# TensorE's order in a pipelined decoder layer: the gate projection split around a transpose, the query projection moved ahead of the gated scores

## The reference

```
x = x + gla(layernorm(x))             # gated linear attention, 16 heads
x = x + cross(layernorm(x), ctx)      # cross attention, 112 + 16 keys
x = x + moe(layernorm(x))             # 4 experts, top 2, capacity 512

gla:   q, k, v = x@Wq.T, x@Wk.T*s, x@Wv.T;  g = x@Wg.T + bg
       o = scan with decay over tokens (as blocked scores here), normed per head
       return silu(g) * o @ Wo.T
cross: q = ln_head(x@Wq + bq);  k, v from ctx, k normed per head
       return (softmax(q k) v, once for 112 keys, once for 16, added) @ Wo + bo
```

## Time and profile before

| | us |
|---|---|
| median of 3 runs | 1132.35 (1131.61 to 1132.56) |
| the profiled execution | 1131.85 |
| its span in the trace | 1130.1 |
| PE busy | 974.3 (86%) |
| DVE, ACT, POOL busy | 716.4, 470.1, 519.7 |
| mean granted clock of TensorE | 0.912 |

### The profile page before, as it was taken

How to read it: one execution, slowest core, us unless ns; L and a number is a source line. 1 busy time by engine, 2 the same in 40 slices (tenths; PEclk the granted TensorE clock), 3 DMA queues, 4 the chain that set the end, 5 groups by cost and what they waited for, 6 DMA issues and landing times.

```text
span 1130.1 us, 19117 instructions
## 1 busy us (share of the span) xinstructions
PE 974.3 (86%) x7225; PEld 570.4 (50%) x7225; DVE 716.4 (63%) x1397; ACT 470.1 (42%) x774; POOL 519.7 (46%) x610
## 2 busy tenths in 40 slices
PE   4699999999999999999999752107899999999994
PEld 2355666666666666666665432103344444444442
DVE  7677867877787778777876445622446446446572
ACT  4544564556555655555554324112233233233210
POOL 2446767666766676667666521277100000002642
PEclk9598999999999999999999875559899999999998
DMA  8340000000000000000000006155534334334583
GB/s 286 115 155 8 8 8 3 7 6 6 1 5 6 6 1 5 6 6 2 4 2 5 1 1 223 49 196 162 115 111 150 112 111 150 111 111 148 170 234 120
DMA packets 43644, 82.73 MB, mean 73 GB/s; under 512 B 12107, under 2 KB 12379, under 8 KB 43601
## 3 DMA queue, kind: packets, MB, share of 16 engines
q1 hardware_dynamic: 37328, 67.45, 18.7%
q0 software_dynamic: 6272, 14.71, 4.2%
HBM read 64.29 MB, written 22.04 MB: 76 GB/s over the span
## 4 chain that ended last, share of the span: by engine, by line
PE 57%; DVE 17%; issue 8%; POOL 7%; DMA 5%; ACT 3%; SPq 2%; POOLq 0%; DVEq 0%
PE ps L988 14%; PE ps L989 13%; PE ps L990 13%; PE ps L1080 5%; PE ps L994 4%; PE ps L1172 3%; POOL xg_scratch L691 3%; POOL xn_all L703 2%; DVE G L1431 2%; PE ps L1183 2%; DVE mx L1536 2%; PE ps L1203 2%; DVE sm L1549 1%; DVE big L1658 1%; DMA xn_all<-y_scratch,idx_get 1%
## 5 line engine op out<-in xcount | busy, mean ns | idle before, releaser
L703 POOL DMA_INDIRECT xn_all<-y_scratch,idx_get x32 | 37.3, 1165 | 257.2 <-DMA y_scratch<-big 241.7
L575 POOL TENSOR_TENSOR hrs<-hve,neg_half 128x16 f32<-128x16 f32 x48 | 139.9, 2914 | 3.8
L962 ACT ACTIVATE big<-ps 128x512 f32<-128x512 f32 x64 | 38.1, 597 | 223.4 <-PE ps L990 223.1
L988 PE MATMUL ps<-w2h,big 128*128 128x512 f16 x256 | 97.7, 381 | 11.0 <-DVE big L1328 11.0
L1723 DVE TENSOR_SCALAR big<-big 128x512 f16<-128x512 f32 x64 | 27.7, 432 | 119.8 <-ACT big L962 119.8
L988 PE MATMUL ps<-big,w1h 128*128 128x512 f16 x256 | 97.0, 379 | 1.5 <-DVE big L1328 1.5
L989 PE MATMUL ps<-w2l,big 128*128 128x512 f16 x256 | 97.5, 381 | 0.0
L990 PE MATMUL ps<-w2h,big 128*128 128x512 f16 x256 | 97.5, 381 | 0.0
L989 PE MATMUL ps<-big,w1h 128*128 128x512 f16 x256 | 97.0, 379 | 0.0
L990 PE MATMUL ps<-big,w1l 128*128 128x512 f16 x256 | 97.0, 379 | 0.0
L1080 PE MATMUL ps<-qeo,kt 32*128 32x64 f32 (+3 forms) x1024 | 72.0, 261 | 8.2 <-DVE scm L1478 8.2
(11 more groups left out here) (291 smaller groups left out, 2636.3 us busy)
## 6 DMA issues: line engine op xcount, KB each, us to landing
wst<-in_w SPq DMA_DIRECT2D x32, 1024.0 KB, 5.3
xg_scratch<-zero SPq DMA_DIRECT2D x16, 256.0 KB, 8.5
big<-xg_scratch SPq DMA_DIRECT2D x4, 1024.0 KB, 7.7
out<-x_all SPq DMA_DIRECT2D x4, 1024.0 KB, 8.7
pr<-in_w_attn SPq DMA_DIRECT2D x3, 1024.0 KB, 8.2
x_all<-in_w_attn SPq DMA_DIRECT2D x3, 1024.0 KB, 10.9
x_all<-in_x SPq DMA_DIRECT2D x1, 3072.0 KB, 11.4
y_scratch<-big SPq DMA_DIRECT2D x3, 1024.0 KB, 5.0
```

What stands on the lines that cost most here:

```text
L575: pool.tensor_tensor(hrs[n][:, :], hve[n][:, :], neg_half[:, :], ALU.pow).then_inc(hdev[n], 1)
L703: pool.indirect_dma_start(out=yg[b], out_offset=None, in_=y_dram, in_offset=bass.IndirectOffsetOnAxis(ap=idx_get[:, k, b:b + 1], axis=0), ...
L962: act.activation(hg[f % 2], psum[f % 2][:, 512:1024], ACT.Gelu, scale=UN).then_inc(hg_r, 1)
L988: nc.tensor.matmul(o, lh, rh, start=first, stop=False)
```

## The change

TensorE's body gets another order; no instruction is added or removed on any engine, and no other engine's order changes. `rows` takes the range of k slices, and gives its signal only with the last of them. `a1_g` is called twice, for k = 0, 1 and k = 2, 3, six matmuls each; `b1_x` comes between. `b1_q`, which was the second step of the next pass on `s[2]`, becomes the last step of the pass on `s[1]` (the same sequence), after `b2_logits` and ahead of the next pass's S0.

```diff
-            def rows(ps, xh, xl, col, done):
+            def rows(ps, xh, xl, col, done, ks=range(KC)):
 
-                for k in range(KC):
+                for k in ks:
                     last = mm3(ps, xh[:, k, :], xl[:, k, :], wh[:, k, col:col + D], wl[:, k, col:col + D], k == 0, k == KC - 1)
-                last.then_inc(done, 1)
+                if k == KC - 1:
+                    last.then_inc(done, 1)
...
-            def a1_g(s):
+            def a1_g(s, ks):
                 b, par, half = s
                 weights(b, 2)
                 after(pe, v_r, b)
-                rows(a1, xth, xtl, C_G, g_ps)
+                rows(a1, xth, xtl, C_G, g_ps, ks)
...
             def body(s):
                 on(s[1], a2_scores, 0)
-                on(s[2], b1_q)
                 on(s[3], b2_turn, 0)
                 on(s[1], a2_scores, 1)
...
                 on(s[3], b2_x3)
-                on(s[0], a1_g)
+                on(s[0], a1_g, range(KC // 2))
                 on(s[1], b1_x)
+                on(s[0], a1_g, range(KC // 2, KC))
                 on(s[3], b2_logits)
+                on(s[1], b1_q)
```

## The result

The changed kernel takes 1180.77 us (median of 4 runs, 1177.96 to 1185.87), the one before 1131.98 (median of 4). The ratio is 1.0441, interval 1.040 to 1.048: slower by 4.4%. The profiled execution took 1177.96 us, its span is 1176.1, against 1131.85 and 1130.1.

The account below looks back on a forecast made before the run. PE was taken as the bound, at half clock for a stretch in most passes. From 1131.85 us: plus 34 for the longer path, minus 21 for old falls, plus 35 for new ones, 1180 us; range 1148 to 1191.

Parts of the forecast that it names:

- b1_x waits: At b1_x, now six matmuls earlier in PE's list: PE idles 1.1 to 1.3 us for xn2, which comes unchanged.
- S1 waits for the mask: At a2_scores 1, covered only by transposes: about 1.1 us idle, 3.70 us from a2_scores 0 to it.
- The path at full clock: PE from b1_x to a2_scores 1: 9.10 us against 6.83, 2.27 us a pass longer, 34 us over 15 paths.
- The old falls go: Half-clock stretches of about 3.4 us, in b1_q: at best all 14 go away, 21 us back.
- New falls, over S1: Clock falls over a2_scores 1 and steps behind: 15 passes, two in three long (2.75 us), others 1.5: 35 us.
- What makes a fall long: A fall just before a2_scores 1 lasts 6.8 us, since that step leaves the clock down; full matmuls of b1_q raised it.
- short falls only: Rival: the clock falls in each pass but is back after 3.4 us: 1167 us, chance 0.30.
- no falls: Rival: dense b1_q next to the thin steps keeps the clock up: 1145 us, chance 0.14.
- the faster one: Rival: the clock stays up and xn2 is there when PE gets to b1_x: 1126 us, chance 0.03.

Follow-up runs that it names:

- e1: The changed kernel with b1_q put back to its old place, so that only the gate projection is split: 1138.64 us, ratio 1.0036 to the kernel before.
- e3: The changed kernel with four more full matmuls of 512 columns in PE's idle time between b2_turn 0 and a2_scores 1: 1141.14 us.
- e6: The changed kernel with eight more thin float32 matmuls (32 rows, 64 columns) between b2_turn 0 and a2_scores 1: 1194.98 us.
- e2: The kernel before with only b1_q moved to after b2_logits, the gate projection left whole: 1176.88 us, ratio 1.0387.
- e4: The kernel before with four more full matmuls of 512 columns ahead of a2_scores 0, where PE is never idle: 1134.72 us, ratio 1.0009.

## Why the prediction held, point by point

Forecast 1180, measured 1180.77, in the range. The direction rested on two waits that the rows of before already priced, and on where the clock would fall.

- *b1_x waits.* Forecast 1.1 to 1.3 us idle, measured 0.98. The reason held: six matmuls earlier in the list, `xn2` comes when it came, 2.82 us after the start of `b2_x3` (316.78 - 313.96), before 2.83 (334.01 - 331.18). e1 shows the price of the split on the pass, 0.86 us at full clock.
- *S1 waits for the mask.* Forecast S0 to S1 3.70 us with 1.1 idle, measured 3.65 with 0.94. The mask's 1.42 us from pass 1 was the right row.
- *The path at full clock.* `b1_x` to S1 was forecast at 9.10 us, measured 316.83 to 325.76 = 8.93. On a whole pass the waits cost 1.94 us (e3), not 2.27: the term was too large by a sixth, 15 x 0.33 = 5 us. The missing part is what `b1_x` could gain, the 0.2 us that I had seen ahead of it and kept for the bound, and the 0.17 us between 9.10 and 8.93, most of it the logits: from their start to that of `b1_q` 0.81 us (319.43 - 318.62) and not 0.98. (The ends of pass without logits are those of passes 1 and 2, not 2 and 3; the sum doesn't change.)
- *The old falls go.* Forecast 21 us back for 14 falls. `b1_q` now runs at 1.00 in the loop (the stretch from 291.80), but only the 13 falls of the passes 4 to 16 went, 20 us; that of pass 2 stayed.
- *New falls, over S1.* Forecast two in three long, 35 us. Measured: all 15 long, each 2.90 us on the pass (2.75 forecast), 43.5 us, or 40.6 for the 14 that weren't there before. That falls come and cost time was right (e3 takes them away with more work, e6 shows that filling the time with thin work doesn't), and the mix was the mis-sized term, by 6 to 8 us.
- *What makes a fall long.* The forecast reasoned from what follows the fall: S1 leaves the clock down, the full matmuls of `b1_q` had brought it back. The runs don't bear this step out. In the profiles of before, e1, e2 and e4 all falls of the passes 4 to 16 come during the scores step (S0, in e2 S1) or just after it. Those within 1.3 us of its start were long, those some 1.5 us or more after it short, whatever followed; at 1.4 us there are two long ones (e2) and a short one (before). In e4 two long ones lie over `b1_q`. In the changed kernel S1 starts within 0.3 us of the fall, from pass 4 on, so all are long; with another length of pass, as in e2, S1 is sometimes nearly over, and the stretch is short.
- The sum can be checked where the traces have both ends, over the twelve passes from pass 4 to 16: waits 12 x 1.94 = 23.3, new falls 12 x 2.90 = 34.8, old falls gone 12 x 1.52 = 18.2 (37.60 - 36.08), together 39.9, the measured 39.9. The three paths before that cost 7.9 us, and after pass 16 1.8 us came back: 46.0, the difference of the spans. The forecast had 34 - 21 + 35 = 48. The waits were 5 us too high and the falls 6 to 8 too low, so it is partly luck that the sum is nearer than its parts.

The rivals: short falls only (1167) is excluded by the 15 stretches of 6.8 us; no falls (1145) is excluded by the same, and e3, where they are taken away, gives 1141; the faster one by the wait of 0.98 us at `b1_x`. The rule of the Trainium skill, page "TensorE: Matmul & The Clock Gate", section "Why this matters for your kernels", that an engine kept busy keeps its clock, doesn't hold here: e6's stretch is busy for 3.20 of 3.20 us ahead of the fall.

Not settled: why the passes of the changed kernel settle where S1 always meets the fall, why e1 and e4 lose some falls and not all, and what sets the length of a fall. That it hangs on where in the pass the clock falls fits all these traces, but is only argued: no run moved that alone.

## What to carry to other kernels

A step that looks like filler may be cover: before moving it, list who is ready just in time behind it (here `xn2` by 0.2 us, the mask by 1.5) and price the bare wait from a place in the trace where it stands alone. Where thin matmuls, transposes and waits stand in a row, look at the granted clock there; put dense work between them (it took the falls away in e3, and only some of them in e4), or move a thin step between dense ones, which gave 1.8% here with the same matmuls. And when a term for the clock enters a sum, say how long the stretch is as well as how often.

## What the runs showed of the hardware that I had not expected

- Adding four useless full matmuls in an idle time of 0.94 us made a kernel 40 us faster (1180.8 to 1141.1), one made no difference (1182.9), and sixteen records of thin ones (32 rows, 64 columns) made it slower (1195.0), although PE had no idle in the 3.2 us ahead of the fall.
- Once down, the clock stayed down for 6.8 us when S1 had just begun or was two thirds done and for 3.4 when it was nearly over (e2); in e4 it stayed down for 6.8 us through twelve full matmuls. S1, transposes and products lose much at half clock, if less than full matmuls: 3.41 against 2.12 us and 1.11 against 0.66, where full matmuls start every 0.43 us instead of 0.22.
- Transposes and products alone brought it up again: in the changed kernel nothing else runs from 329.1 to the rise at 332.7. So did transposes alone: in the kernel before PE is idle for 9.56 us, runs 16 of them at 0.50, and has 1.00 after them (the transposes, their stretch, the next one).

```profile
692.61 3.54 PE L1243 MATMUL ps<-ident,big 128*128 128x128 f32 x16 [9.56 <-DVE big L1640]
...
692.60:695.80 3.20, 3.19 (x15) 3.20 (x16) 2.24 (x18) 1.53 (x3) 0.00 (x0) 0.50 1.06 406
696.00:699.20 3.20, 0.15 (x2) 0.00 (x0) 2.29 (x2) 3.08 (x6) 0.00 (x0) 1.00 1.06 406
```

The Trainium skill, page "TensorE: Matmul & The Clock Gate", section "Part 4: PE-mode transpose", says that the full clock doesn't engage for matmuls in transpose mode; the trace does not agree for these float32 transposes, made by `nc.tensor.transpose`.
